# A wait ahead of GpSimd's angle work in the opening of a fused two-layer kernel

## The chip, the cores and the metric

The kernel runs on one core of a Trainium2 chip. The metric is the device time of one execution in microseconds. Three timed runs of the kernel before gave 691.99, 692.20 and 692.33, median 692.2. A profiled execution, from which all rows below are taken, took 692.8.

## The reference

The input x has 4 x 2048 tokens of 512 values (8192 tokens). Two layers follow, each with a residual and a layer norm:

```python
ab, AB = xis, exp(xis)
rfs(v) = 1/sqrt(512) * AB * exp(v @ (ab * gs).T - 0.5 * sum(v*v) * ab*ab)   # 512 features
x = layernorm(x + rfs(x) @ rfs(input_weights).T)
real = x @ cos(theta + theta_noise)
imag = x @ sin(phi + phi_noise)
x = layernorm(x + sqrt(real*real + imag*imag))
```

gs, the input weights, theta, phi and the two noises are 512 x 512 in float32. The cosine is computed as a sine of the angle plus pi/2. [...]

## The kernel before, in words

Tokens are worked in 16 blocks of 512. Every product is done in three matmuls of float32r: high part by high part, high by low and low by high. So each operand needs a high part (ScalarE rounds it) and a low part (VectorE subtracts the high part from the whole). A 512 x 512 matrix lies as four chunks c of 128 rows.

For a block there are the stages *project* (exponents of the features; TensorE, lines 1021 to 1031), the feature exponentials on ScalarE (`features`, line 645), their low parts on VectorE (`split_features`, line 1315, which counts up `F_made`), *mix* (the product with W, lines 1082 to 1092), the first residual and norm, transposes, *phase* (the products with cosine and sine), and the second norm.

Each engine has one queue, written out by hand in program order, and engines wait for each other on counting semaphores. Steady blocks run in loops; the opening does not. In the opening the constants are made while the first blocks are already worked:

- VectorE (from line 1378) makes eight exponents in the order W 0, W 1, W 2, block 0 chunk 0, W 3, block 0 chunks 1, 2, 3. Behind each it makes the low part of the one before: `scale_W` (line 1365) for W, `split_features` for block 0. So the third low part of block 0's features is made behind the last of these exponents, and it sets `F_made` to 3. Then come one small transpose, four low parts of xT of block 1 (`split_lo`, line 1320), and `first_step` (line 1501).
- `first_step` on VectorE mixes residuals (L1454), means (L1467), two exponents (L1312) and low parts of transposes and of cosine and sine (L1307) with `reduce_angle` (line 1394). For theta that is one scalar_tensor_tensor (L1401) and a clamp (L1405) per chunk, for phi one more add (L1398).
- GpSimd (from line 431) does the other part of each angle: `add_noise` (line 443) issues a DMA that adds the noise in place, and `count_turns` (line 448) takes, per chunk of theta, three tensor_scalars (L454, L457, L464) and one tensor_tensor (L467), and per chunk of phi two tensor_scalars (L457, L462). Its last instruction in a chunk counts up `turns_made`, for which `reduce_angle` waits. The order of its queue is: four noise DMAs of theta, theta chunks 0 to 2, four noise DMAs of phi, theta chunk 3 (line 523), the four chunks of phi (line 528), `make_damp`, and then the sums of cosine and sine (`sum_chunks`, line 491), which wait for all sines.
- ScalarE makes the sines (`sine`, line 667) from the clamped angles; TensorE's mix takes chunk c of the features when `F_made` is at c + 1.

The noise DMAs are the only transfers in GpSimd's queue. The loads of theta, phi and x are in SP's queue.

Of the kernel before, what the change touches and what calls it, by code (L numbers as in the profile page):

```python
# [42 lines left out]
def build(nc, xT, x, wT, xis, gsT, theta, phi, theta_noise, phi_noise, out):  # L43
# [5 lines left out]
    C = D // P  # L49
# [13 lines left out]
    with ExitStack() as ctx:  # L63
# [162 lines left out]
        project_done, expo_made, exp_done, F_made = sem("project_done"), sem("expo_made"), sem("exp_done"), sem("F_made")  # L226
# [204 lines left out]
        def _(pool):  # L431
# [11 lines left out]
            def add_noise(buf, c, noise, loaded, n):  # L443
                pool.wait_ge(loaded[c], 16)
                pool.dma_start(buf[:, c, :], by_chunk(noise)[:, c, :], accum_op=ALU.add).then_inc(noise_added[n + c], 16)

            steps = 0
            def count_turns(angles, whole_turns, c, n, offset):

                nonlocal steps  # L450
                angle, turns = angles[:, c, :], whole_turns[:, c, :]
                pool.wait_ge(noise_added[n + c], 16)
                if offset:
                    pool.tensor_scalar(angle, angle, offset, 1.0, ALU.add, ALU.mult).then_inc(trig_step, 1)  # L454
                    steps += 1
                    pool.wait_ge(trig_step, steps)
                pool.tensor_scalar(turns, angle, 1.0 / (2 * np.pi), ROUNDER, ALU.mult, ALU.add).then_inc(trig_step, 1)  # L457
                steps += 1
                pool.wait_ge(trig_step, steps)
                if n:  # L460

                    pool.tensor_scalar(turns, turns, -ROUNDER, -TWO_PI_A, ALU.add, ALU.mult).then_inc(turns_made, 1)  # L462
                    return
                pool.tensor_scalar(turns, turns, -ROUNDER, -TWO_PI_A, ALU.add, ALU.mult).then_inc(trig_step, 1)  # L464
                steps += 1
                pool.wait_ge(trig_step, steps)
                pool.tensor_tensor(angle, angle, turns, ALU.add).then_inc(turns_made, 1)  # L467

            for c in range(C):
                add_noise(theta_angle, c, theta_noise, theta_loaded, 0)  # L470
            for c in range(C - 1):
                count_turns(theta_angle, theta_turns, c, 0, HALF_PI)
            for c in range(C):
# [1445 lines left out]
```

## Time and profile before

| | |
|---|---|
| timed runs, median | 692.2 us |
| profiled execution | 692.8 us |
| its span | 691.0 us |
| TensorE busy | 681.0 us (99%) |
| VectorE busy | 582.2 us (84%) |
| ScalarE busy | 482.9 us (70%) |
| GpSimd busy | 165.1 us (24%) |
| mean granted TensorE clock | 0.997 |

The profile names TensorE PE, VectorE DVE, ScalarE ACT and GpSimd POOL. A line of a timeline gives the start and the duration in us, the engine, the line of the kernel, the operation, what it writes and reads with the shapes, and in brackets how long the engine stood idle before it and what ended that. A duration runs from the moment at which the engine took up the instruction, so it holds any waiting inside the engine. An instruction can be taken up some 0.08 us before the one ahead of it ends. TensorE's busy time is modelled and its share is not its distance from the peak. Many low parts share the line L1307, so they are told apart by the tile that they write.

### The profile page before, as it was taken

Reading aid. Unit: us, or ns where it says so; the run is one execution under the profiler, and the core shown is the slowest. Engines: PE = TensorE matmul, PEld = TensorE weight load, DVE = VectorE, ACT = ScalarE, POOL = GpSimd, SP = SyncE. Lnnn points to the kernel's source line nnn. Section 1 sums busy time; section 2 is a strip of 40 time slices with the busy share of each in tenths; the row PEclk is TensorE's granted clock in tenths of the full one; section 3 lists DMA queues with packets and bytes.
Section 4 is the critical chain, followed back from the end, with each engine's and each line's share of the span. In section 5 each row is a group of like instructions: output and inputs, shape, how many; then the busy total and the mean of one; then the engine's idle time right before and its main releaser. Section 6 shows DMA issues by size and latency. Waiting matters only on the chain.

```text
span 691.0 us, 10119 instructions
## 1 busy us (share of the span) xinstructions
PE 681.0 (99%) x3008; PEld 561.3 (81%) x3008; DVE 582.2 (84%) x935; ACT 482.9 (70%) x800; POOL 165.1 (24%) x236
## 2 busy tenths in 40 slices
PE   9999999999999999999999999999999999999995
PEld 7788888878888888888888888888888888888884
DVE  6889899888979798797969879797887979889787
ACT  7768998387585757668585776758667675875466
POOL 2672304103012040301304031030302104030205
PEclk9999999999999999999999999999999999999998
DMA  8861031360825527072452806355181543606142
GB/s 298 250 138 61 16 111 73 108 212 25 228 84 130 173 82 238 15 227 88 125 182 67 251 16 185 119 129 190 41 239 54 156 147 111 208 24 175 36 117 93
DMA packets 106727, 90.24 MB, mean 131 GB/s; under 512 B 62800, under 2 KB 77136, under 8 KB 106704
## 3 DMA queue, kind: packets, MB, share of 16 engines
q1 hardware_dynamic: 103776, 86.30, 41.6%
q0 software_dynamic: 1152, 2.10, 1.8%
q10 hardware_dynamic: 1776, 1.57, 0.7%
q8 instruction: 10, 0.16, 0.1%
q14 instruction: 13, 0.11, 0.1%
HBM read 58.46 MB, written 31.49 MB: 130 GB/s over the span
## 4 chain that ended last, share of the span: by engine, by line
PE 82%; DVE 8%; issue 5%; ACT 3%; DMA 1%; POOL 0%; SPq 0%; POOLq 0%; DVEq 0%; ACTq 0%
PE token_ps L1085 7%; PE token_ps L1087 7%; PE token_ps L1086 7%; PE token_ps L1198 6%; PE token_ps L1199 6%; PE token_ps L1200 6%; PE project_ps L1024 4%; PE project_ps L1026 4%; PE project_ps L1025 4%; PE project_ps L1200 4%; PE project_ps L1199 4%; PE project_ps L1198 4%; PE turn_ps L1026 3%; PE turn_ps L1025 3%; PE turn_ps L1024 3%
## 5 line engine op out<-in xcount | busy, mean ns | idle before, releaser
L506 POOL TENSOR_TENSOR plain_late<-z,plain_late 128x1024 f32<-128x1024 f32 x13 | 31.3, 2410 | 289.3 <-ACT plain_late L758 289.3
L1085 PE MATMUL token_ps<-W_hi,F_hi 128*128 128x512 f32 x240 | 93.5, 389 | 0.3 <-DVE F_lo L1307 0.3
L1087 PE MATMUL token_ps<-W_hi,F_lo 128*128 128x512 f32 x240 | 93.4, 389 | 0.0
L1086 PE MATMUL token_ps<-W_lo,F_hi 128*128 128x512 f32 x240 | 93.4, 389 | 0.0
L764 ACT ACTIVATE o_tile<-plain_late,shift,rstd 128x512 f32<-128x512 f32 x56 | 42.8, 809 | 56.5 <-POOL shift L519 53.1
L650 ACT ACTIVATE F_hi<-plain_expo,ab 128x512 fp32r<-128x512 f32 x62 | 44.5, 717 | 22.4 <-DVE plain_expo L1312 22.3
L758 ACT ACTIVATE plain_late<-plain_late 128x1024 f32<-128x1024 f32 x28 | 29.6, 1058 | 42.2 <-POOL plain_late L502 39.3
L1024 PE MATMUL project_ps<-xT_hi,gs_hi 128*128 128x512 f32 x144 | 56.8, 394 | 0.1
L1026 PE MATMUL project_ps<-xT_hi,gs_lo 128*128 128x512 f32 x144 | 56.1, 390 | 0.0
L1025 PE MATMUL project_ps<-xT_lo,gs_hi 128*128 128x512 f32 x144 | 56.1, 389 | 0.0
L1307 DVE TENSOR_TENSOR xT_lo<-plain_xT_lo,xT_hi 128x1024 fp32r<-128x1024 f32 x28 | 49.4, 1801 | 6.4 <-ACT xT_hi L678 6.4
L1085 PEld LDWEIGHTS token_ps<-W_hi,F_hi 128*128 128x128 f32 x240 | 45.1, 188 | 10.1 <-issue 0.7
L1087 PEld LDWEIGHTS token_ps<-W_hi,F_lo 128*128 128x128 f32 x240 | 45.1, 188 | 9.4
L1086 PEld LDWEIGHTS token_ps<-W_lo,F_hi 128*128 128x128 f32 x240 | 45.1, 188 | 9.3
L1307 DVE TENSOR_TENSOR zT_lo<-plain_zT_lo,zT_hi 128x1024 fp32r<-128x1024 f32 x27 | 33.1, 1226 | 17.8 <-ACT zT_hi L853 17.8
L1307 DVE TENSOR_TENSOR F_lo<-plain_F_lo,F_hi 128x1024 fp32r<-128x1024 f32 (+1 forms) x38 | 42.2, 1138 | 3.1 <-ACT plain_F_lo L651 3.1
L1454 DVE TENSOR_TENSOR z<-token_ps,x_tok 128x512 f32<-128x512 f32 x60 | 40.9, 685 | 3.9 <-PE token_ps L1087 1.1
L1024 PE MATMUL turn_ps<-xT_hi,gs_hi 128*128 128x512 f32 x112 | 44.0, 393 | 0.0
L651 ACT ACTIVATE plain_F_lo<-plain_expo,ab 128x512 f32<-128x512 f32 x62 | 43.9, 709 | 0.0
L1198 PE MATMUL token_ps<-T_hi,zT_hi 128*128 128x512 f32 x112 | 43.7, 390 | 0.2 <-ACT plain_late L862 0.2
L1026 PE MATMUL turn_ps<-xT_hi,gs_lo 128*128 128x512 f32 x112 | 43.6, 389 | 0.0
L1025 PE MATMUL turn_ps<-xT_lo,gs_hi 128*128 128x512 f32 x112 | 43.6, 389 | 0.0
(347 smaller groups left out, 1932.3 us busy)
## 6 DMA issues: line engine op xcount, KB each, us to landing
x_tok<-in_x SPq DMA_DIRECT2D x16, 1024.0 KB, 6.3
out_tokens<-o_tile SPq DMA_DIRECT2D x62, 256.0 KB, 3.0
plain_xT_lo<-in_xT SPq DMA_DIRECT2D x14, 1024.0 KB, 8.0
turned_pair<-plain_late SPq DMA_DIRECT2D x104, 128.0 KB, 2.9
plain_late<-turned_pair SPq DMA_DIRECT2D x26, 512.0 KB, 3.9
norm_bc<-token_norms SPq DMA_DIRECT2D x15, 256.0 KB, 3.1
z<-in_wT ACTq DMA_DIRECT2D x4, 256.0 KB, 5.2
plain_T_hi<-in_gsT SPq DMA_DIRECT2D x4, 256.0 KB, 5.4
```

What stands on the lines that cost most here:

```text
L650: nc.scalar.activation(F_hi[:, j, :], exponents, ACT.Exp, scale=ab[:, j:j + 1]).then_inc(exp_done, 1)
L651: nc.scalar.activation(F_raw[:, j, :], exponents, ACT.Exp, scale=ab[:, j:j + 1]).then_inc(exp_done, 1)
L1024: nc.tensor.matmul(o, gs_hi[:, c, cols], rhs_hi[:, c, :], start=(c == 0), stop=False)
L1025: nc.tensor.matmul(o, gs_hi[:, c, cols], rhs_lo[:, c, :], start=False, stop=False)
L1026: return nc.tensor.matmul(o, gs_lo[:, c, cols], rhs_hi[:, c, :], start=False, stop=(c == C - 1))
L1085: nc.tensor.matmul(o, F_hi[:, c, cols], W_hi[:, c, :], start=(c == 0), stop=False)
L1086: nc.tensor.matmul(o, F_hi[:, c, cols], W_lo[:, c, :], start=False, stop=False)
L1087: return nc.tensor.matmul(o, F_lo[:, c, cols], W_hi[:, c, :], start=False, stop=(c == C - 1))
L1198: nc.tensor.matmul(o, left[0][i], right[0][i], start=(i == 0 and not onto), stop=False, skip_group_check=onto)
L1199: nc.tensor.matmul(o, left[0][i], right[1][i], start=False, stop=False, skip_group_check=onto)
L1200: last = nc.tensor.matmul(o, left[1][i], right[0][i], start=False, stop=(i == H - 1), skip_group_check=onto)
L1307: return tt(dst, whole, hi.bitcast(F32), ALU.subtract)
```

## The change

One line is added to GpSimd's queue: a wait until `F_made` has reached C - 1 = 3. It stands behind the issues of theta's noise and ahead of the first `count_turns`. Nothing else is changed; everything of GpSimd's queue that lies behind this point, phi's noise DMAs among it, lies behind the wait.

```diff
             for c in range(C):
                 add_noise(theta_angle, c, theta_noise, theta_loaded, 0)
+            pool.wait_ge(F_made, C - 1)
             for c in range(C - 1):
                 count_turns(theta_angle, theta_turns, c, 0, HALF_PI)
             for c in range(C):
```

## Rows read from the trace of the kernel before

**Rows 1.** The page's head and first part: busy us, share of the span, instructions.
```profile
span 691.0 us, 10119 instructions
PE 681.0 (99%) x3008; PEld 561.3 (81%) x3008; DVE 582.2 (84%) x935; ACT 482.9 (70%) x800; POOL 165.1 (24%) x236
```

**Rows 2.** The chain that ended last, 31 to 93 us: start, us, what.
```profile
31.44 0.47 PE token_ps L1085
...
65.17 0.44 DVE plain_late L1405
...
92.23 0.75 DVE plain_expo L1312
```

**Rows 3.** GpSimd's timeline, 22 to 50 us.
```profile
22.62 0.62 POOL L454 TENSOR_SCALAR plain_T_hi<-plain_T_hi 128x512 f32<-128x512 f32 x1 [5.37 <-DMA plain_T_hi<-in_theta_noise]
...
24.72 1.29 POOL L467 TENSOR_TENSOR plain_T_hi<-plain_T_hi,plain_T_lo 128x512 f32<-128x512 f32 x1
25.98 1.06 POOL L454 TENSOR_SCALAR plain_T_hi<-plain_T_hi 128x512 f32<-128x512 f32 x1
...
35.38 3.55 POOL L445 DMA_DIRECT2D plain_late<-in_phi_noise  x4
37.62 2.50 POOL L454 TENSOR_SCALAR plain_T_hi<-plain_T_hi 128x512 f32<-128x512 f32 x1
...
44.08 0.67 POOL L462 TENSOR_SCALAR plain_T_lo<-plain_T_lo 128x512 f32<-128x512 f32 x1
...
48.54 0.68 POOL L462 TENSOR_SCALAR plain_T_lo<-plain_T_lo 128x512 f32<-128x512 f32 x1
```

**Rows 4.** VectorE's timeline, 21 to 49 us.
```profile
21.94 0.75 DVE L1368 SCALAR_TENSOR_TENSOR W_lo<-plain_late,W_scale,W_hi 128x512 fp32r<-128x512 f32 x1
...
24.73 1.83 DVE L1368 SCALAR_TENSOR_TENSOR W_lo<-plain_late,W_scale,W_hi 128x512 fp32r<-128x512 f32 x1
...
30.16 1.13 DVE L1307 TENSOR_TENSOR F_lo<-plain_F_lo,F_hi 128x512 fp32r<-128x512 f32 x1
...
31.87 0.68 DVE L1307 TENSOR_TENSOR F_lo<-plain_F_lo,F_hi 128x512 fp32r<-128x512 f32 x1
...
36.76 0.69 DVE L1307 TENSOR_TENSOR xT_lo<-plain_T_hi,xT_hi 128x512 fp32r<-128x512 f32 x1 [0.31 <-ACT xT_hi L618]
...
37.97 1.10 DVE L1307 TENSOR_TENSOR xT_lo<-plain_T_hi,xT_hi 128x512 fp32r<-128x512 f32 x1
38.99 0.68 DVE L1307 TENSOR_TENSOR xT_lo<-plain_T_hi,xT_hi 128x512 fp32r<-128x512 f32 x1
...
44.20 0.83 DVE L1467 TENSOR_SCALAR z<-z,neg_mean 128x512 f32<-128x512 f32 x1
...
48.66 0.73 DVE L1312 SCALAR_TENSOR_TENSOR plain_expo<-norm_bc,neg_half_ab,project_ps 128x512 f32<-128x512 f32 x1
```

**Rows 5.** VectorE by groups, 40.9 to 49.35 us: busy us, mean ns, idle before.
```profile
L1467 DVE TENSOR_SCALAR z<-z,neg_mean 128x512 f32<-128x512 f32 x4 | 2.8, 724 | 0.2 <-ACT o_tile L686 0.2
L1401 DVE SCALAR_TENSOR_TENSOR plain_T_hi<-plain_T_lo,plain_T_hi 128x512 f32<-128x512 f32 x2 | 1.9, 930 | 0.0
...
L1405 DVE TENSOR_SCALAR plain_T_hi<-plain_T_hi 128x512 f32<-128x512 f32 x1 | 0.7, 729 | 0.0
```

**Rows 6.** VectorE by groups, 49.3 to 66.1 us.
```profile
L1307 DVE TENSOR_TENSOR zT_lo<-turn_ps,zT_hi 128x512 fp32r<-128x512 f32 x3 | 2.1, 686 | 0.4 <-ACT zT_hi L692 0.4
...
L1405 DVE TENSOR_SCALAR plain_late<-plain_late 128x512 f32<-128x512 f32 x4 | 1.7, 427 | 0.1
```

**Rows 7.** Timeline of VectorE and GpSimd, 72.8 to 75.1 us.
```profile
72.89 1.97 DVE L1307 TENSOR_TENSOR F_lo<-plain_F_lo,F_hi 128x512 fp32r<-128x512 f32 x1 [0.85 <-ACT plain_F_lo L651]
...
74.38 1.62 POOL L496 TENSOR_TENSOR plain_late<-plain_late 128x512 f32<-128x512 f32 x1
...
74.78 1.78 DVE L1307 TENSOR_TENSOR F_lo<-plain_F_lo,F_hi 128x512 fp32r<-128x512 f32 x1
```

**Rows 8.** Phi's noise DMAs, 30 to 60 us: from issue to landing.
```profile
DMA to landing us min/median/max: 4.2/6.3/7.4
```

## The prediction

> **What bounds the kernel now.** The page first [rows 1]: TensorE is busy for 99% of the span, so in the steady blocks a late GpSimd costs nothing. The change touches only the opening, and TensorE's share is an average over everything, so I read the chain of waits for the opening next [rows 2]. It shows TensorE standing idle for the low part of the first block's second feature chunk (it resumes at 31.44), then TensorE to about 53, then VectorE with hardly a break to the clamp of phi's last angles (65.17 + 0.44 = 65.6), and on through ScalarE, the feature splits, the sums and the centring to the exponent at 92.23. From there TensorE is full. So what moves VectorE's clamp at 65.6 should move the end by as much; I see no transfer in that part of the chain.
>
> Then the timelines of GpSimd and VectorE side by side [rows 3, 4]. The two do not run freely beside each other. GpSimd's add takes 24.72 to 26.01. VectorE's W_lo, issued at 24.73, takes 1.83 us where the same instruction took 0.75 at 21.94, and ends 0.55 after the add. The other way, GpSimd's multiply at 25.98 takes 1.06 where the one at 22.62 took 0.62: it ends 0.48 after W_lo. So each holds, for a whole instruction, something that the other needs. A GpSimd add that had to wait ends 1.15 after VectorE's instruction (74.38 + 1.62 against 72.89 + 1.97), and there the two alternate: the add gets in between two back-to-back splits, and the second takes 1.78 [rows 7]. A tensor_scalar of VectorE ends 0.28 after GpSimd's multiply (44.20 + 0.83 = 45.03 against 44.08 + 0.67 = 44.75). VectorE's instructions with an operand in PSUM (exponents, residuals, splits of the transposes) show no such stretching; I count them as free. One meeting, with VectorE's queue full (splits follow every 0.60), thus costs it 0.48 + 0.55 - 0.60 = 0.43 behind a multiply and 1.15 + 0.55 - 0.60 = 1.10 behind an add.
>
> **The change, part by part.** One wait goes into GpSimd's queue, behind the issues of theta_noise. Queued behind it: 12 instructions for theta chunks 0 to 2, four DMA issues of phi_noise (35.38, 3.55 us of GpSimd), 4 instructions for theta chunk 3, 8 for phi, then damp. It is released by the third low part, which ends now at 31.87 + 0.68 = 32.55 [rows 4]. SP's and ScalarE's queues get nothing new; who waits for the held-back work is VectorE, for the angles.
>
> *What goes.* W_lo at 24.73 loses 1.83 - 0.75 = 1.08, the split at 30.16 loses 1.13 - 0.68 = 0.45. Followed op by op at uncontended durations (W_lo to 25.48, exponent to 26.13, ScalarE's Exp and W_hi to 27.71, next W_lo to 28.50, exponent to 29.15, second split to 29.75, exponent to 30.40, third split to 31.31) the release comes 1.24 earlier, and TensorE's idle place closes: 0.28 and the slow first matmul behind it, 0.4 to 0.5 us [rows 2].
>
> *What comes.* GpSimd starts at 31.35 instead of 22.62. Walked against VectorE with the numbers above: theta 0 to 35.1, theta 1 to 39.5, theta 2 to 43.3, DMA issues to 46.9, theta 3 to 50.4, phi to 58.3 (now 48.54 + 0.68 = 49.2 [rows 3]). VectorE pays, by stretch:
>
> 1. The four xT_lo splits, from 36.76 now, ending at 38.99 + 0.68 = 39.67. ScalarE is 1.4 earlier, so they start at 35.3 and alone would end at 37.8. But theta 1 lies on them: three multiplies and an add, 0.25 (a part of one) + 0.43 + 0.43 + 1.10 = 2.2. They end at 40.0, 0.35 later than now; TensorE's project starts as much later, and the 0.5 us won ahead of it is spent waiting.
> 2. From there to 49.4. Now VectorE pays 4 x (0.724 - 0.427) = 1.19 on the means, 2 x (0.930 - 0.680) = 0.50 on theta's reductions and 0.30 on a clamp, 2.0 in all [rows 5]. Afterwards GpSimd spends 3.55 us of this stretch on DMA issues, and the walk gives 0.31 + 0.51 + 0.10 + 0.41 = 1.3. VectorE catches up 0.35 + 0.2: the second exponent ends at 49.16, now 48.66 + 0.73 = 49.39.
> 3. 49.4 to 58.4. Now nothing is paid: clamps take 427 ns, splits 686, and VectorE idles 0.4 once, for ScalarE's copy of a transpose [rows 6]. Afterwards theta 3's add stands ahead of theta 1's reduction (1.15, with no overlap behind it), and phi's multiplies fall on clamps (0.29, 0.30, 0.30), on theta 3's reduction (0.42) and on a split of the cosine (0.43): 2.9. Of it 1.74 lies ahead of the idle 0.4 and fills it. So 2.9 - 0.2 - 0.4 = 2.3; with the gaps between dependent instructions the walk has 2.24.
> 4. From 58.4 GpSimd is done, as now, and VectorE's queue runs at today's durations, 2.2 late. GpSimd's sums follow the sines and shift with them.
>
> The sum: the profiled execution took 692.8 (span 691.0 and 1.8 around it), with 2.2 more 695.0. The timed runs lie a little lower, so their median becomes 692.2 + 2.2 = 694.4. No operation is added; work that lay on VectorE's waits for ScalarE comes to lie where VectorE is the bound.
>
> *Bounds.* Unknown is who gets in where both queues are full. From below: GpSimd's multiplies never hold VectorE up, as at 38.99, where a split took 0.68 while the multiply of 37.62 stood waiting for 2.50 [rows 3, 4]. Stretches 1 and 3 are then free and TensorE and ScalarE bound the gain, -0.9. From above: the DMA issues. The split at 37.97 took 1.10 while they ran, 0.42 more, one of four. I take 0, since the walk puts the new issues mostly over exponents and residuals; 0.42 on each of two tensor_scalars is the other end, +3.0. I take the walk's +2.2 as nearest to the rows: 24.73, 30.16, 44.20 and 74.78 follow it, 38.99 alone does not.
>
> **A rule weighed.** During the DMA issues of now, one of VectorE's tensor_tensors was stretched by 0.42 and the others were not [rows 4]. The Trainium skill ("SBUF — State Buffer", sections "SBUF: two separate sides" and "Who interferes with whom") says the reverse pair matters: descriptors of DMAs in GpSimd's queue can't be written while VectorE runs a two-port instruction, while it infers that a tensor_tensor does not disturb them. By this the two tensor_scalars at 44 to 45 would lengthen the issues by up to 0.9; GpSimd's queue slides along VectorE's and the sum stays within 2.2 to 2.3. For its second half the trace shows a stretched tensor_tensor, and the measurement decides.
>
> **Rivals.** *A, VectorE keeps what it holds.* Where its instructions follow back to back GpSimd waits them out (38.99 for it; 74.78 and 30.16 against). Place: stretches 1 and 3; price -0.9, so 691.3, not slower than before. It decides if the four xT_lo splits keep about 0.68 each.
> *B, a late phi.* The noise issues come 8 us later and land up to 7.4 after their issue [rows 8], and GpSimd may be held up more than I think. VectorE wants phi's first turns at 58.8, the walk has them at 52.2: a cover of 6.6, and beyond it every us is one on the path. Before that, a later GpSimd still meets more of VectorE's full stretch: with 8 us for the issues instead of 3.55 the walk gives +3.7, 695.9. Against: the issues took 3.55 in spite of VectorE's splits.
> *C, slack downstream.* Half of the 2.2 is taken up between 66 and 92 by ScalarE's or TensorE's own order: +1.1, 693.3. Against: the chain is closed through that stretch [rows 2].
> *D, the wait does nothing,* since GpSimd waits for noise anyway. It doesn't: it starts at 22.62, 8.7 ahead of the release [rows 3].
>
> **How the numbers follow.** Forecast 0.64, A 0.16, B 0.08, C 0.10, D 0.02. The forecast alone spans 693.6 to 695.2 (GpSimd 0.3 us earlier or later and issues of 3 to 6 us gave +1.8 to +2.8, and a little on either side). The range reaches into A and B: 692.0 to 695.7. A measurement of this kernel can tell 0.2%, 1.4 us, from no change. Slower by more: forecast but for its edge, and B, 0.70. Within: C, D, most of A, that edge, 0.24. Faster: the far end of A, 0.06.
>
> **What would show it.** W_lo near 24.7 at 0.75, the third split ended near 31.3, no idle of TensorE inside the mix, GpSimd's first theta instruction just behind. The four xT_lo splits over 4 us in all instead of 2.9; theta 1's reduction near 49 at 1.8; clamps at 50 to 58 at 0.73 instead of 0.43; phi done at 58; the last phi clamp ended near 67.8. I am wrong if that clamp ends at or before 65.6, or if it ends at 67.8 and the exponent of 92.23 has not moved with it.

## The result, and the profile after

The changed kernel takes 694.70 us in the median of seven timed runs (694.50 to 695.32), the kernel before 692.26 in seven (691.99 to 693.12). The ratio is 1.0033, with a 95% interval of 1.0024 to 1.0043: slower by 2.3 us (1.7 to 3.0). Forecast was 694.4. The profiled execution took 694.8, 2.0 more than the one of before.

The page of after: GpSimd's and TensorE's busy time hardly move, VectorE's rises by 2.5 us with not one instruction more.

```profile
span 693.0 us, 10120 instructions
PE 681.9 (98%) x3008; PEld 561.6 (81%) x3008; DVE 584.7 (84%) x935; ACT 483.7 (70%) x800; POOL 166.1 (24%) x236
```

From the wait on, every line number is one higher. The chain that ended last answers to [rows 2]: TensorE's resumption at 31.44 is gone from it (until 40 the chain runs through ScalarE and VectorE), and the other two steps are there, each 2.0 later.

```profile
67.17 0.44 DVE plain_late L1406
...
94.22 0.75 DVE plain_expo L1313
```

GpSimd's timeline answers to [rows 3]. The bracket shows the new wait. The first instruction that it holds back came at 22.62 before; the last one ends at 57.77 + 0.94 = 58.7 instead of 49.2.

```profile
31.07 0.62 POOL L454 TENSOR_SCALAR plain_T_hi<-plain_T_hi 128x512 f32<-128x512 f32 x1 [14.07 <-DVE F_lo L1308]
...
42.90 3.62 POOL L445 DMA_DIRECT2D plain_late<-in_phi_noise  x4
...
48.95 1.85 POOL L467 TENSOR_TENSOR plain_T_hi<-plain_T_hi,plain_T_lo 128x512 f32<-128x512 f32 x1
...
57.77 0.94 POOL L462 TENSOR_SCALAR plain_T_lo<-plain_T_lo 128x512 f32<-128x512 f32 x1
```

VectorE's timeline answers to [rows 4]. The first two rows are what the change wins: W_lo in 0.75 instead of 1.83, the third low part ended at 30.97 instead of 32.55. Then come the four xT_lo splits, every one stretched, where one was before. The clamp at 43.55 takes 0.73 instead of 0.43 while GpSimd runs nothing but the DMA issues of 42.90. The clamp of theta 1 at 49.67 waits 1.0 for the add at 48.95.

```profile
24.45 0.75 DVE L1369 SCALAR_TENSOR_TENSOR W_lo<-plain_late,W_scale,W_hi 128x512 fp32r<-128x512 f32 x1
...
30.28 0.69 DVE L1308 TENSOR_TENSOR F_lo<-plain_F_lo,F_hi 128x512 fp32r<-128x512 f32 x1
...
34.94 0.97 DVE L1308 TENSOR_TENSOR xT_lo<-plain_T_hi,xT_hi 128x512 fp32r<-128x512 f32 x1 [0.31 <-ACT xT_hi L619]
35.83 1.09 DVE L1308 TENSOR_TENSOR xT_lo<-plain_T_hi,xT_hi 128x512 fp32r<-128x512 f32 x1
36.85 1.09 DVE L1308 TENSOR_TENSOR xT_lo<-plain_T_hi,xT_hi 128x512 fp32r<-128x512 f32 x1
37.86 1.77 DVE L1308 TENSOR_TENSOR xT_lo<-plain_T_hi,xT_hi 128x512 fp32r<-128x512 f32 x1
...
43.55 0.73 DVE L1406 TENSOR_SCALAR plain_T_hi<-plain_T_hi 128x512 f32<-128x512 f32 x1
...
49.67 1.41 DVE L1406 TENSOR_SCALAR plain_T_hi<-plain_T_hi 128x512 f32<-128x512 f32 x1
```

VectorE by groups from 40.9 to 49 answers to [rows 5]: the means are a little cheaper (644 ns against 724).

```profile
L1468 DVE TENSOR_SCALAR z<-z,neg_mean 128x512 f32<-128x512 f32 x4 | 2.5, 644 | 0.2 <-ACT o_tile L687 0.2
L1402 DVE SCALAR_TENSOR_TENSOR plain_T_hi<-plain_T_lo,plain_T_hi 128x512 f32<-128x512 f32 x2 | 1.9, 930 | 0.0
...
L1406 DVE TENSOR_SCALAR plain_T_hi<-plain_T_hi 128x512 f32<-128x512 f32 x1 | 0.7, 730 | 0.0
```

And from 49.6 to 58.2, the stretch in which nothing was paid before [rows 6]: clamps of 957 ns in the mean for 427, reductions and splits above 800 for 680, and the 0.4 us of idle time ahead of zT_lo gone.

```profile
L1406 DVE TENSOR_SCALAR plain_T_hi<-plain_T_hi 128x512 f32<-128x512 f32 x3 | 2.9, 957 | 0.1
L1402 DVE SCALAR_TENSOR_TENSOR plain_T_hi<-plain_T_lo,plain_T_hi 128x512 f32<-128x512 f32 x3 | 2.4, 815 | 0.0
L1308 DVE TENSOR_TENSOR cos_lo<-plain_T_lo,cos_hi 128x512 fp32r<-128x512 f32 x3 | 2.4, 812 | 0.0
L1308 DVE TENSOR_TENSOR zT_lo<-turn_ps,zT_hi 128x512 fp32r<-128x512 f32 x3 | 2.0, 677 | 0.0
L1399 DVE TENSOR_TENSOR plain_late<-plain_late,plain_T_lo 128x512 f32<-128x512 f32 x1 | 1.1, 1095 | 0.0
```

### The profile page after: what moved, and what is told of

Same layout as the page of the kernel before. It is cut to its first block, busy times and chain, and to the rows that moved or that the text cites. A ratio compares the mean times of both kernels' runs of the same rounds, so it can differ in the third digit from the quotient of the medians.

```text
span 693.0 us, 10120 instructions
## 1 busy us (share of the span) xinstructions
PE 681.9 (98%) x3008; PEld 561.6 (81%) x3008; DVE 584.7 (84%) x935; ACT 483.7 (70%) x800; POOL 166.1 (24%) x236
## 3 DMA queue, kind: packets, MB, share of 16 engines
q1 hardware_dynamic: 103776, 86.30, 41.3%
## 4 chain that ended last, share of the span: by engine, by line
PE 82%; DVE 10%; issue 5%; ACT 3%; POOL 0%; POOLq 0%; DVEq 0%
PE token_ps L1088 7%; PE token_ps L1087 7%; PE token_ps L1086 7%; PE token_ps L1199 6%; PE token_ps L1200 6%; PE token_ps L1201 6%; PE project_ps L1201 4%; PE project_ps L1200 4%; PE project_ps L1199 4%; PE project_ps L1025 4%; PE project_ps L1027 4%; PE project_ps L1026 4%; PE turn_ps L1027 3%; PE turn_ps L1026 3%; PE turn_ps L1025 3%
## 5 line engine op out<-in xcount | busy, mean ns | idle before, releaser
L1027 PE MATMUL project_ps<-xT_hi,gs_lo 128*128 128x512 f32 x144 | 56.1, 390 | 0.0
L1026 PE MATMUL project_ps<-xT_lo,gs_hi 128*128 128x512 f32 x144 | 56.1, 389 | 0.0
L1455 DVE TENSOR_TENSOR z<-token_ps,x_tok 128x512 f32<-128x512 f32 x60 | 40.9, 685 | 3.9 <-PE token_ps L1088 1.1
```

The costliest lines, as they stand in the source:

```text
L1026: nc.tensor.matmul(o, gs_hi[:, c, cols], rhs_lo[:, c, :], start=False, stop=False)
L1027: return nc.tensor.matmul(o, gs_lo[:, c, cols], rhs_hi[:, c, :], start=False, stop=(c == C - 1))
```

## The experiments

The theory to test is that of the prediction, called turn-taking here: GpSimd's and VectorE's instructions of certain kinds exclude each other for their whole length and alternate, so the change moved collisions from where VectorE had time to where it has none. The rivals are that lateness itself costs (the angles or phi's noise come too late), that the wait costs, and that the early collisions are the ones that matter. "Last clamp" below is the end of VectorE's last phi clamp in the profiled execution, 65.60 before and 67.60 after. That instant moves by some tenths from one execution to the next, as the first loads land earlier or later, so the timed ratio goes first where the two differ.

**e1_null.** The wait in its place, but for something that is made before GpSimd can start anyway.

```diff
-            pool.wait_ge(F_made, C - 1)
+            pool.wait_ge(W_made, 1)
```

> The wait stands in the same place, but asks for the first low part of W, made 1 us before GpSimd's noise lands (GpSimd started its first theta instruction at 22.62 in the trace of before). Turn-taking theory and every other theory that works through the time at which GpSimd starts: like before, 692.3, GpSimd's first theta instruction at 22.6, VectorE's last phi clamp ended at 65.6. A theory by which the wait itself costs (an extra semaphore wait in GpSimd's queue, code that is laid out otherwise): like after, 694.7.

Measured 692.74, ratio 1.0001 (0.9992 to 1.0010), last clamp 65.61. No cost of the wait as an instruction can be seen.

**e2_first.** The wait for the first low part instead of the third.

```diff
-            pool.wait_ge(F_made, C - 1)
+            pool.wait_ge(F_made, 1)
```

> The wait asks for the first low part of the block's features instead of the third: GpSimd starts near 26.8 instead of 31.1. Turn-taking walk (two-operand VectorE instruction ends 0.55 after GpSimd's, GpSimd's 0.48 or 1.15 after VectorE's): phi done near 54.3, so only about the first half of the stretch 49 to 58 is contended: last phi clamp 0.8 later than before, 66.4, time 693.1. A rival by which any delay of GpSimd is handed on one for one to the angles: 4.3/8.5 of the loss, 693.5. A rival by which only the DMAs' new place counts: no sharp number, between 692.3 and 694.7.

Measured 693.28, ratio 1.0011 (1.0002 to 1.0020), that is 0.8 us slower; last clamp 66.41, 0.8 later. GpSimd started at 27.30 and ended phi at 54.32, and by then theta 3's clamp was free again: the groups from 49.3 to 60 show a smaller mean for the same clamps than after.

```profile
L1402 DVE SCALAR_TENSOR_TENSOR plain_T_hi<-plain_T_lo,plain_T_hi 128x512 f32<-128x512 f32 x3 | 2.5, 828 | 0.0
L1406 DVE TENSOR_SCALAR plain_T_hi<-plain_T_hi 128x512 f32<-128x512 f32 x3 | 1.9, 627 | 0.1
```

A delay of 4.7 us costs a third of what 8.5 us cost, in the timed runs and in the trace. A loss handed on one for one would have been over half, 1.3 us. The interval, 0.1 to 1.4 us, doesn't rule that out by itself; e6 and e8 below do.

**e3_xT.** The wait for the last low part of block 1's xT.

```diff
-            pool.wait_ge(F_made, C - 1)
+            pool.wait_ge(xT_lo_made, 2 * C)
```

> The wait asks for the last low part of the second block's xT: GpSimd starts near 37.9, 7 us later than in the changed kernel. Turn-taking alone would add little to the changed kernel's loss, as the 12 instructions of theta 3 and phi meet the same full queue of VectorE: 694.7 to 695.3. With the cover of phi's turns used up (the walk has the last of them made at 63.9 and the changed kernel wants them near 66) VectorE begins to wait for GpSimd and turn-taking lasts to the end of the stretch: clamp at 70.4, 4.8 later than before, time 697.1. The four xT_lo splits are free in both cases and end near 37.8.

Measured 697.16, ratio 1.0071 (1.0057 to 1.0085); last clamp 69.70. The splits are free and end at 37.75, so the early gain and more is in hand, and yet the kernel is the slowest of all: here VectorE has begun to wait for GpSimd's results, 0.6 us at 41.3 for theta 0's turns and 1.2 us at 56.2 for theta 3's. That is rival B's mechanism, at places earlier than I had put it (theta, not phi). These are VectorE's waits from 40 to 66.

```profile
DVE plain_T_hi L1402 <- POOL plain_T_hi L467: 1.8, 2, 1.2
DVE zT_lo L1308 <- ACT zT_hi L693: 0.6, 1, 0.6
```

In the changed kernel VectorE never waits for GpSimd's results, only inside its instructions. So of the two ways in which a late GpSimd can cost, waits inside VectorE's instructions and waits for GpSimd's results, the change meets the first alone.

**e4_w3.** The kernel before, with only the add of theta's first chunk held back past W_lo.

```diff
+                if c == 0:
+                    pool.wait_ge(W_made, 3)
                 pool.tensor_tensor(angle, angle, turns, ALU.add).then_inc(turns_made, 1)
```

> The kernel before with another, shorter wait: only GpSimd's add of theta's first chunk is held back until W_lo 2 is made (from 24.72 to 25.4). Turn-taking walk: W_lo 2 takes 0.75 instead of 1.83, the second low part of the features ends 0.8 earlier, the last phi clamp 0.3 earlier: 691.9 to 692.0. A rival by which the early stretch has slack anyway: 692.3. One by which every delay of GpSimd costs: 692.5 or more.

Measured 693.08, ratio 1.0007 (0.9998 to 1.0016), last clamp 65.73: no gain, and my number is missed. It lies where the expectation put the rival by which every delay of GpSimd costs; e7 and e8 below speak against that one. W_lo did take 0.75, but the add, held back to 25.75, fell on the very next split instead, which took 1.25 for 0.68. Theta's noise had also landed at 20.0 in this execution, so the rest of GpSimd's queue met VectorE elsewhere, and its fourth add caught the first clamp, which took 1.40 instead of 0.73:

```profile
26.34 1.25 DVE L1309 TENSOR_TENSOR F_lo<-plain_F_lo,F_hi 128x512 fp32r<-128x512 f32 x1
...
41.80 1.78 POOL L469 TENSOR_TENSOR plain_T_hi<-plain_T_hi,plain_T_lo 128x512 f32<-128x512 f32 x1
42.47 1.40 DVE L1407 TENSOR_SCALAR plain_T_hi<-plain_T_hi 128x512 f32<-128x512 f32 x1
```

A collision removed by hand came back 1.5 us later, and another 18 us later. My 0.3 us was within what the placing of such a queue does by chance.

**e5_last12_small.** After, with the 12 instructions of theta 3 and phi on 8 columns; the other columns of the turns (the whole turns to be taken off each angle) are left out.

```diff
+            pool.memset(theta_turns, 0.0).then_inc(turns_cleared, 1)
...
-                angle, turns = angles[:, c, :], whole_turns[:, c, :]
+                columns = 8 if n or c == 3 else B
+                angle, turns = angles[:, c, :columns], whole_turns[:, c, :columns]
```

> The changed kernel with the 12 GpSimd instructions of theta 3 and phi made on 8 columns instead of 512 (the rest of these turns is left out, so the values are not the reference's; a memset of the turns at the start, with GpSimd idle, gives them a value). The wait, the place of the DMAs and theta 0 to 2 stay. Turn-taking: stretch 49 to 58 is free again, clamps 0.43, last phi clamp near 65.5, time 692.2 to 692.8; the splits of xT_lo still take over 4 us. A theory in which the loss comes from the late DMAs of phi's noise or from theta 0 to 2: 694.7 stays.

Measured 693.72, ratio 1.0011 (1.0002 to 1.0020), last clamp 66.54. Two thirds of the loss are gone and all seven clamps from 49 on take 0.43, as turn-taking asks, but the number is above its range; the last clamp is too, in part because the third low part came 0.8 later here (31.76) than in the trace of after. Beside the stretched xT_lo splits, which stay, the trace shows ScalarE waiting 0.24 for the next block's x, and VectorE 0.28 for a sine behind that. That cost I had not counted; e11 and e12 come back to it.

**e6_last12_memset.** After, with the same 12 instructions as memsets of the same 128x512 turns: most of the lateness stays, the reading goes. The turns are left out.

```diff
+                if n or c == 3:
+                    for k in range(2 if n else 4):
+                        last = k == (1 if n else 3)
+                        pool.memset(turns, 0.0).then_inc(turns_made if last else trig_step, 1)
...
+                    return
```

> The changed kernel with the same 12 instructions replaced by memsets of the same 128x512 turns: they write and read nothing (the values are not the reference's). Turn-taking over reads alone: VectorE's two-operand instructions (reductions, splits) between 49 and 58 take 0.68 again, its clamps (two-port) may still be stretched to 0.7: last phi clamp 0 to 1 us later than before, time 692.3 to 693.3. Turn-taking for any instruction of GpSimd: like after, 694.7 less what shorter memsets save. A theory of lateness: 694.7. The Trainium skill (SBUF — State Buffer, Who interferes with whom) says the first: two SBUF inputs contend only with a GpSimd instruction that reads SBUF.

Measured 693.37, ratio 1.0012 (1.0003 to 1.0021), last clamp 65.16. By the timed runs 0.8 us of the loss of 2.3 are left. The profiled execution, 692.69, was among the fastest of the eleven and doesn't show this 0.8, so its clamp decides nothing. GpSimd is busy as late as 56.08 (49.2 before, 58.7 after), and VectorE's groups from 49 to 58 are nearly those of before:

```profile
L1316 DVE TENSOR_TENSOR cos_lo<-plain_T_lo,cos_hi 128x512 fp32r<-128x512 f32 x4 | 2.7, 681 | 0.0
...
L1410 DVE SCALAR_TENSOR_TENSOR plain_T_hi<-plain_T_lo,plain_T_hi 128x512 f32<-128x512 f32 x3 | 2.0, 679 | 0.0
L1414 DVE TENSOR_SCALAR plain_T_hi<-plain_T_hi 128x512 f32<-128x512 f32 x3 | 1.4, 465 | 0.1
```

So without the reading, a late GpSimd doesn't stretch the two-operand instructions at all. The Trainium skill ("SBUF — State Buffer", section "Who interferes with whom") has this rule, that a VectorE instruction with two SBUF inputs meets only GpSimd instructions that read SBUF; by this run's 681 and 679 ns the trace agrees. The same section says that VectorE in what it calls a two-port mode, which a tensor_scalar can enter, contends with GpSimd, and makes no such exception for GpSimd's writers. One mean beside a memset agrees:

```profile
46.79 0.80 POOL L456 MEMSET plain_T_lo<- 128x512 f32 x1
47.04 0.83 DVE L1476 TENSOR_SCALAR z<-z,neg_mean 128x512 f32<-128x512 f32 x1
```

The clamps beside memsets, 465 ns in the mean, hardly do.

**e7_before_small and e8_after_small.** All 24 instructions on 8 columns, without and with the wait (the edit of e5, without its condition; the turns of the other columns are left out).

> The kernel before with all 24 GpSimd instructions on the angles made on 8 columns (values not the reference's). Turn-taking: nothing is stretched from 24 to 66; the walk has the last phi clamp at 64.7, 0.9 earlier, time 691.4: all that any placing of this work can win. A rival by which the early collisions are the larger part, as the change supposes: 690.5 or less.

> As the last one, with the wait for F_made at 3 in place: 24 small instructions behind the wait (values not the reference's). Turn-taking: the same 691.4, since the late start costs nothing once nothing collides; the angles' turns are all made by 41. A theory in which the wait or the lateness costs by itself: 2.4 above the one without the wait.

Measured 691.74, ratio 0.9990 (0.9981 to 0.9999), and 691.82, ratio 0.9989 (0.9979 to 0.9998). The pair says three things. All collisions in the kernel before are worth 0.7 us of time (0.1 to 1.3), although VectorE's instructions are stretched there by 1.08 + 0.45 + 0.24 + 0.42 + 2.0 = 4.2 us (0.24 is a split at 33.35 that took 0.92, and 0.42 fell beside the DMA issues): most of that falls where it would have waited anyway. Without them it waits for ScalarE and TensorE instead, as VectorE's waits of e7 from 30 to 66 show. The first of the three was 1.0 in the kernel before, the second 2.0, the third absent. And with nothing to collide, a GpSimd held back by 10 us (its first instruction at 31.38 for 21.42) costs nothing that the timed runs can tell.

```profile
DVE zT_lo L1310 <- ACT zT_hi L695: 3.1, 3, 1.5
DVE norm_row L1420 <- ACT unused L597: 2.2, 1, 2.2
DVE plain_expo L1315 <- PE project_ps L1029: 0.7, 2, 0.5
```

The traces of the pair are less alike than the times: the last clamp is at 64.86 in e7 and at 65.52 in e8, of which 0.3 is there from the third low part on. In e8 the transfer of the block's norms, issued right behind phi's noise, took 6.6 us to land instead of 3.2, and VectorE waited for it:

```profile
DVE plain_expo L1316 <- DMA norm_bc<-token_norms: 3.1, 1, 3.1
```

**e9_dma_first.** After, with phi's noise DMAs ahead of theta's counts.

```diff
             pool.wait_ge(F_made, C - 1)
+            for c in range(C):
+                add_noise(phi_angle, c, phi_noise, phi_loaded, C)
             for c in range(C - 1):
                 count_turns(theta_angle, theta_turns, c, 0, HALF_PI)
-            for c in range(C):
-                add_noise(phi_angle, c, phi_noise, phi_loaded, C)
```

> The changed kernel with phi's four noise DMAs moved from behind theta 2 to right behind the wait, so issued near 31 to 35 as in the kernel before (35.4), and theta's counts start 3.6 later. Turn-taking walk: xT_lo splits end 39.8, the first clamps of 42 to 46 meet more of GpSimd, the last phi clamp ends 0.4 later than in the changed kernel (68.0), time 694.9 to 695.1. The block's x, loaded in 10.8 us in the changed kernel and in 5.3 before, lands in 5.3 again, and nothing of the time goes back. A theory in which the DMAs' late place (phi's noise and x sharing the queues between 43 and 56) makes the loss: time falls towards 692.5.

Measured 695.58, ratio 1.0036 (1.0023 to 1.0050), last clamp 68.64. The DMAs are back at 32 and x lands in 5.1, and the kernel is no faster than after. The median lies above my number; the ratio alone would give 694.8, just below its range. So the late place of the DMAs is not the loss as a whole. A part of some tenths isn't ruled out, since theta's counts start later here, for which I had reckoned 0.4 more. Here is x from issue to landing, first after, then e9:

```profile
DMA to landing us min/median/max: 10.8/10.8/10.8
```

```profile
DMA to landing us min/median/max: 5.1/5.1/5.1
```

**e10_early_memset.** The kernel before, with the 12 instructions of theta 0 to 2 as 18 memsets.

```diff
+                if not n and c < C - 1:
+                    for k in range(6):
+                        last = k == 5
+                        pool.memset(turns, 0.0).then_inc(turns_made if last else trig_step, 1)
...
+                    return
```

> The kernel before with the 12 GpSimd instructions of theta 0 to 2 replaced by 18 memsets of the same turns, which read nothing and fill about the same time (values not the reference's): the early collisions alone are gone, all the rest of GpSimd's queue runs as in the kernel before. Turn-taking: W_lo 0.75, third low part 31.0 to 31.3, the four xT_lo splits from 35.3, but the last phi clamp only 0.3 to 0.9 earlier (64.7 to 65.3), because TensorE and ScalarE bound what a faster start can hand on: time 691.4 to 692.0. A rival by which the early collisions are worth what they stretch, 1.08 + 0.45 + 0.24 = 1.8: 690.6.

Measured 692.42, ratio 0.9994 (0.9985 to 1.0003), last clamp 65.73. W_lo takes 0.75 and the third low part ends at 31.32; by the time the gain cannot be told from none. The freed GpSimd reached theta 3 at 33 and fell on the xT_lo splits, which took 4.72 in all:

```profile
36.84 1.60 POOL L475 TENSOR_TENSOR plain_T_hi<-plain_T_hi,plain_T_lo 128x512 f32<-128x512 f32 x1
```

```profile
35.29 4.72 DVE L1315 TENSOR_TENSOR xT_lo<-plain_T_hi,xT_hi 128x512 fp32r<-128x512 f32 x4 [0.31 <-ACT xT_hi L626]
```

So this run takes the early collisions away and brings others. The net is 0.4 us by the ratio, which the interval doesn't tell from nothing, and the clamp did not come earlier. A price of 1.8 for the early collisions, the only ones that the change removes, is out by e7 too, where all of them together are worth 0.7.

**e11_memset_again and e12_memset_dma_first.** The kernel of e6 once more, and the same with e9's edit, for the 0.8 us that e5 and e6 left over.

> The kernel with the last 12 instructions as memsets once more (values not the reference's), as the partner of the next one on the same chip: again 0.7 to 0.9 us above the kernel before, 693.3, with the block's x landing some 10.4 us after its issue.

> The same with phi's noise DMAs moved to right behind the wait (values not the reference's). If the 0.8 us left over after the reading was taken out come from phi's noise and x sharing the queues at 43 to 56 (x in 10.4 instead of 5.3, ScalarE on the edge of waiting for it): time back to 692.5, x in 5.3. If they come from theta 0 to 2 on the xT_lo splits and the clamps of 42 to 46, which stay: the same as its partner or, as theta's counts now start 3.6 later, up to 0.5 more.

Measured 693.18, ratio 1.0013 (1.0004 to 1.0022), and 692.86, ratio 1.0007 (0.9998 to 1.0016). x lands in 10.9 and 5.1, and ScalarE's wait of 0.2 for it is there in the one and not in the other. The time falls by 0.3, inside both intervals. A part of the remainder may be the loads that share the queues; the rest would be theta 0 to 2 on the splits. This stays open.

No version that does all of the work beat the kernel before. What another placing of it could win is bounded by e7, an estimate: 0.1% below the kernel before.

## Why the prediction was right

**The bound.** The chain through VectorE's last phi clamp held: clamp and exponent moved by 2.0 and 2.0, the span by 2.0. Rival C, slack downstream, is out: nothing is taken up between 66 and 92. D is out by the trace: GpSimd's first count starts at 31.07 and not at 22.62. B is out for this change: phi's first turns were made at 52.76, and VectorE takes them up at 58.15.

**What goes.** W_lo lost 1.08 and the second low part 0.45 as forecast, and TensorE no longer idles inside the mix. The release came at 30.97 where I had 31.31; W_lo had already started 0.3 earlier (24.45 for 24.73), which is of this execution and not of the change.

**Stretch 1.** Four splits from 34.94 to 39.64, 4.71 us; free they take 3 x 0.60 + 0.68 = 2.48. The walk's 2.2 of stretching is 2.23 in the trace. They end where they did before (39.67), not 0.35 later, by the same 0.3 of the start, which is used up here: from 41.0 to 44.2 the two traces agree within 0.03. TensorE idles 0.21 for them. The alternation was there in each of the four, and that puts rival A out: its test was 0.68 each. The row at 38.99, on which A and my lower bound rested, was weaker than I read it. The multiply of 37.62 stood in the queue behind the DMA issues, which ended at 35.38 + 3.55 = 38.93, so VectorE did not hold it up before then. In e9 it is the same: a split at 35.52 took 0.69 while a multiply stood behind issues that ended at 35.57.

**Stretch 2.** Paid: 4 x (0.644 - 0.427) = 0.87 on the means, 0.50 on reductions, 0.30 on a clamp, 1.7 in all. The walk had 1.3 and the kernel before paid 2.0. The term was too small by about 0.35. The walk gives its four parts without naming the instructions, so which one was missing can't be read off for certain. But 0.30 of what was paid is the clamp at 43.55, beside nothing but the DMA issues, and for those the prediction had put 0; it weighed up to 0.42 on each of two tensor_scalars as the other end. In e3 a clamp at 49.38 took 0.74, again beside the issues alone, while in e5 and e6 the clamps beside the issues took 0.43 and 0.49. What decides is open. The issues themselves took 3.62 beside two tensor_scalars, for 3.55 before, so the lengthening by up to 0.9 that the prediction weighed did not come; and the stretched split at 37.97, which it set against the rule's second half, is the other direction, VectorE slowed during the issues, and says nothing on that.

**Stretch 3.** Paid: 3 x (0.957 - 0.427) = 1.59 on clamps, 3 x (0.815 - 0.680) = 0.41 on reductions, 0.41 on a split of the cosine, 0.41 on the first add of phi, 2.8 in all for 2.9. The addresses were partly wrong. Theta 3's add fell on theta 1's clamp (1.41), not on its reduction (1.8 forecast), since both instructions were taken up within 0.01 us of each other and VectorE got in first. The total hardly depended on that: VectorE's next instruction paid 0.98 where 1.15 was forecast. That fits with a sum over a full queue being easier to forecast than a single collision, as e4's.

**The sum** was 2.2 in the walk; the trace gave 2.0 and the timed ratio 2.3. In the trace, VectorE comes to the second exponent's end 0.35 earlier than before (49.03 for 49.39), pays 2.8 and saves the idle 0.35: 2.1. That this lies so close to the walk is luck in part, for the early start of 0.3 covered the 0.35 that stretch 2 lacked; without it the trace would come to some 2.3 by my estimate, which is what the timed runs gave. That collisions with GpSimd's reads make most of the loss is shown by the timed runs: e5 and e6, which take those of theta 3 and phi away, lose 0.8 instead of 2.3, e6 with most of the lateness kept; and e8, which keeps the wait and takes all away, loses nothing. The 0.8 is not resolved: theta 0 to 2 on the splits of xT_lo stay in both, and so do the late DMAs.

**What I missed.** I put the DMA issues over free instructions, and one of them, the clamp at 43.55, was not free. Nor did I see their data: between 43 and 56 phi's noise shares the queues with the next block's x, whose landing doubles from 5.3 to 10.8 us (45.3 + 10.8 = 56.1, with ScalarE taking it up at 56.08). In the changed kernel the cover just sufficed; in e5 it did not. And rival B's place was wrong, as e3 shows: the turns that come late are theta's.

## What to carry to other kernels

Before GpSimd's work is moved out of the way of a critical instruction, look at where the whole queue behind it lands. Where VectorE was busy without a break here, each of its 128x512 instructions with two operands in SBUF, and each tensor_scalar, paid 0.3 to 1.1 us for a GpSimd instruction that it met. A stretched instruction costs time only where its engine has no wait coming up; count the idle time ahead of the next wait first, and the stretched durations second. And a queue that is sped up or slowed down at its head collides elsewhere with what follows, as in e4 and e10, so a single collision is no target.

## What the runs showed of the hardware

- A VectorE instruction that finds one of GpSimd ahead of it ends 0.55 us (two SBUF operands) or 0.28 (tensor_scalar, 128x512) after it; a GpSimd tensor_scalar that finds VectorE ahead ends 0.48 after it, an add 1.15. With both queues full they alternated: four splits in a row at 0.97, 1.09, 1.09 and 1.77.
- During GpSimd's DMA issues, with nothing else of GpSimd at work as far as the traces show, some of VectorE's instructions were stretched and others not: splits at 1.10 (before, 37.97; e4, 36.64) among others at 0.68, and clamps at 0.73 and 0.74 (after, e3) among others at 0.43 and 0.49 (e5, e6). What decides is open.
- Memsets of GpSimd leave two-operand instructions at 0.68. They stretched tensor_scalars to 0.83 (a mean in e6, e11 and e12) and 0.78 (a clamp in e11), and hardly (0.43 to 0.52) in other places; I don't know what decides.
- Instructions with an operand in PSUM ran at 0.67 to 0.75 beside any GpSimd instruction, in all traces.
- The transfer of a block's norms took 6.2 and 6.6 us to land where it was issued within 0.4 us behind the issues of the four noise DMAs (e4, e8), 4.2 in the kernel before (2.0 behind), and 3.0 to 3.3 where the noise was issued 4 us or more ahead, or later.
- Four noise DMAs of 256 KB each that overlapped the load of 1 MB of x made it take 10.4 to 10.9 us in four runs, against 5.0 to 5.7 where they did not overlap, and 7.6 where they did in part.
